# Third stage: the two rotary parts of the keys added by an accumulating transfer on GpSimd's queue

## The chip, the cores and the metric

The kernel runs on one core of one Trainium2 chip. The metric is the device time of one launch in microseconds (us).

## The reference

Three parts follow each other, on 64 sequences of 64 tokens of 128 numbers: a self-attention with 16 heads, a cross-attention on a context with a padding mask, and a stack of six layers (the third stage here). The change is in the stack's attention:

```python
def attn_layer(x, Wqkv, qs, ksc, Wo):
    q, k, v = jnp.split(x @ Wqkv, 3, -1)          # 16 heads of 64 each
    q = l2norm(q) * qs
    k = l2norm(k) * ksc
    q = q * cos * scale + rotate_half(q) * sin * scale
    k = k * cos * inv + rotate_half(k) * sin * inv
    out = local_attention(q, k, v)                # window of 32, softmax
    return out.transpose(0, 2, 1, 3).reshape(b, n, INNER) @ Wo
...
for i in range(DEPTH):                            # 6
    x = attn_layer(shift_tokens(x), ...) + x
    x = ffn_layer(shift_tokens(x), ...) + x
```

What matters is the sum in the line of `k`: one product with the cosines plus one with the sines. The kernel writes the two products into two buffers and adds them.

## The kernel before

The 4096 tokens lie in 32 tiles of 128 (two sequences each). The third stage works through 32 tiles times 6 layers, so 192 tile-steps; `turns` runs 192 + 7 turns, and in turn i every engine works at tiles i, i-1, ... down to i-7, each at another step of the chain. Each engine has its own `turn` function, which lists its steps in a fixed order; the engines meet by semaphores alone. Nothing is planned at run time, so an engine that waits at one step holds back all that stand behind it in its list.

The way of one tile's keys through the stage, with the lines of the kernel before:

- TensorE, `queries_keys` (L1044, matmuls at L1041): four 128x512 products, two of them keys, into PSUM.
- ScalarE, `squares` (L1248), then VectorE, `squares_summed` (L1361) and `seeded` (L1369 to L1373): the sums of squares by head and a first guess at the inverse roots.
- VectorE, `rotary` (L1346): the products with cosines and sines, from PSUM into `R[:, KEYS, 0, :]` and `R[:, KEYS, 1, :]`, each 128 x 1024 fp32. It counts `s.rotated`.
- GpSimd, `inverse_lengths` (L1494 to L1502): three Newton steps on 32 columns, each instruction waiting for the one ahead of it.
- GpSimd, `keys_added` (L1451): two additions of 128x512 that put the second part onto the first.
- GpSimd, in its next turn, `keys_scaled` (L1459): two multiplications of 128x512 by the inverse lengths, in place.
- TensorE, in its next turn, `keys_turned` (L1062, transposes at L1014), and ScalarE's `keys_out` (L1222); then the scores.

GpSimd's list of a turn is this, and its order is the order of its queue:

```python
keys_scaled(i - 1, k - 1, 0)
keys_scaled(i - 1, k - 1, 1)
scores_scaled(i - 2, k - 2, 0)
probs_scaled(i - 3, k - 3, 0)
scores_scaled(i - 2, k - 2, 1)
probs_scaled(i - 3, k - 3, 1)
inverse_deviation(i - 5, k - 5)
inverse_lengths(i, k)
keys_added(i, 0)
keys_added(i, 1)
```

`scores_scaled` (L1465) and `probs_scaled` (L1471) are multiplications of 128x512 for the softmax of older tiles: ScalarE's `exponents` (L1261) wait for the first, TensorE's `probs_turned` for the second. `inverse_deviation` (L1478 to L1483) makes the factors of the feed-forward's normalisation, for which ScalarE's `normalised` (L1271) waits; it needs VectorE's `statistics` (L1356). `R` has one buffer: VectorE's next key products wait until TensorE has turned the old ones (`s.k_turned`).

The transfers of the third stage are issued by SyncE: per tile-step six of 16 to 32 KB between SBUF buffers (`ystat`, `ys`), and once in each layer the weights of the next. GpSimd issues no transfer.

Of the kernel before, what the change touches and what calls it, by code (L numbers as in the profile page):

```python
# [24 lines left out]
ALU = mybir.AluOpType  # L25
# [26 lines left out]
def hold(eng, held):  # L52


    eng.sem_inc(held, 1)
# [818 lines left out]
QUERIES, KEYS = 0, 1  # L874
# [4 lines left out]
def turns(eng, turn, n):  # L879

    for i in range(n + LAST):
        turn(i, i % 4)


def inside(t, n):

    return not isinstance(t, int) or 0 <= t < n
# [12 lines left out]
def local(nc, sem, m):  # L900
# [10 lines left out]
    s = Names()  # L911
# [29 lines left out]
    with nc.Block() as block:  # L941
# [494 lines left out]
        @block.gpsimd  # L1436
        def _(pool):
            tt = nc.gpsimd.tensor_tensor

            def wide(small):  # L1440
                return small.unsqueeze(2).to_broadcast([128, 8, HD])

            def by_head(ap):
                return ap.rearrange("p (n k) -> p n k", k=HD)

            def keys_added(t, j):
                if inside(t, N):
                    if j == 0:
                        pool.wait_ge(s.rotated, 4 * t + 4)
                    at = slice(j * 512, (j + 1) * 512)  # L1450
                    tt(m.R[:, KEYS, 0, at], m.R[:, KEYS, 0, at], m.R[:, KEYS, 1, at], ALU.add).then_inc(s.k_added, 1)  # L1451

            def keys_scaled(t, k, j):
                if inside(t, N):
                    pool.wait_ge(s.k_added, 2 * t + j + 1)
                    if j == 0:
                        pool.wait_ge(s.lengths, 12 * t + 12)
                    part = by_head(m.R[:, KEYS, 0, j * 512:(j + 1) * 512])
                    tt(part, part, wide(m.rn[:, k % 4, 16 + 8 * j:24 + 8 * j]), ALU.mult).then_inc(s.k_scaled, 1)  # L1459

            def scores_scaled(t, k, a):
                if inside(t, N):
                    pool.wait_ge(s.less, 2 * t + a + 1)
                    part = by_head(m.P[:, k % 2, a * 512:(a + 1) * 512])
                    tt(part, part, wide(m.rn[:, k % 4, a:16:2]), ALU.mult).then_inc(s.scaled, 1)  # L1465

            def probs_scaled(t, k, a):
                if inside(t, N):
                    pool.wait_ge(s.inverse, 2 * t + a + 1)
                    part = by_head(m.P[:, k % 2, a * 512:(a + 1) * 512])  # L1470
                    tt(part, part, wide(m.inv_sum[:, k % 2, 8 * a:8 * a + 8]), ALU.mult).then_inc(s.normal, 1)  # L1471

            def inverse_deviation(t, k):
                if inside(t, N):
                    one = slice(k % 2, k % 2 + 1)
                    pool.wait_ge(s.var, t + 1)
                    hold(pool, held)
                    nc.gpsimd.tensor_scalar(m.vare[:, :], m.mv[:, k % 2, 1:2], EPS, None, ALU.add).then_inc(s.vare, 1)  # L1478
                    pool.wait_ge(s.vare, t + 1)
                    tt(m.rstd[:, one], m.vare[:, :], m.minus_half[:, :], ALU.pow).then_inc(s.pow, 1)  # L1480
                    pool.wait_ge(s.pow, t + 1)
                    hold(pool, held)
                    nc.gpsimd.tensor_scalar(m.nmr[:, one], m.mv[:, k % 2, 0:1], m.rstd[:, one], -1.0, ALU.mult, ALU.mult)\  # L1483
                        .then_inc(s.rstd, 1)

            def inverse_lengths(t, k):
                if inside(t, N):
                    pool.wait_ge(s.seed, 3 * t + 3)
                    y = m.seed[:, k % 2, :].bitcast(FP32)
                    for step in range(3):  # L1490
                        done = 12 * t + 4 * step
                        if step:
                            pool.wait_ge(s.lengths, done)
                        tt(m.rn_a[:, :], y, y, ALU.mult).then_inc(s.lengths, 1)  # L1494
                        pool.wait_ge(s.lengths, done + 1)
                        tt(m.rn_b[:, :], m.rn_a[:, :], m.ssm[:, k % 2, :], ALU.mult).then_inc(s.lengths, 1)
                        pool.wait_ge(s.lengths, done + 2)
                        hold(pool, held)
                        nc.gpsimd.tensor_scalar(m.rn_a[:, :], m.rn_b[:, :], -0.5, 1.5, ALU.mult, ALU.add)\
                            .then_inc(s.lengths, 1)  # L1500
                        pool.wait_ge(s.lengths, done + 3)
                        tt(m.rn[:, k % 4, :], y, m.rn_a[:, :], ALU.mult).then_inc(s.lengths, 1)  # L1502
                        y = m.rn[:, k % 4, :]

            def turn(i, k):
# [5 lines that stand above are left out]
                probs_scaled(i - 3, k - 3, 1)  # L1511
                inverse_deviation(i - 5, k - 5)
                inverse_lengths(i, k)
                keys_added(i, 0)
                keys_added(i, 1)

            turns(pool, turn, N)


# [48 lines left out]
```

## Time and profile before

| | |
|---|---|
| median of 2 runs | 3672.97 us (3669.88 to 3676.06) |
| the profiled execution | 3669.16 us |
| its span, first to last instruction | 3667.4 us |
| TensorE busy | 3570.1 us (97%) |
| VectorE, ScalarE, GpSimd busy | 2809.8, 2926.9, 2596.7 us |
| mean granted TensorE clock | 0.991 of 2.4 GHz |

The profiled execution's own time and its span differ by 1.8 us. Busy time doesn't say which engine sets the end: an engine at 97% may be held by another, and one at 71% may be the one that all wait for in some stretch. For that the waits, the chain that ended last and the order of one turn have to be read. In the rows, PE is TensorE, PEld its weight loads, DVE VectorE, ACT ScalarE, POOL GpSimd, SP SyncE and SPq SyncE's DMA queue.

### The profile page before, as it was taken

What the parts mean: (1) busy time and instruction counts of PE and PEld (TensorE: products, weight loads), DVE (VectorE), ACT (ScalarE), POOL (GpSimd) and SP (SyncE); (2) the same over time, 40 slices, a digit from 0 to 9 for tenths busy, and PEclk for the clock granted to TensorE, in tenths of its full rate; (3) what the DMA queues carried; (4) which work ended last, traced back from release to release, by engine and by line L of the source; (5) the groups of instructions that cost most, each with busy time, mean ns of one, the idle gap of its engine ahead of it and who ended that gap; (6) DMA issues with size and microseconds to landing.
All of it is one profiled execution on the core that took longest, in us unless ns stands there. A gap on an engine that the chain in (4) does not pass through costs nothing.

```text
span 3667.4 us, 125829 instructions
## 1 busy us (share of the span) xinstructions
PE 3570.1 (97%) x51141; PEld 2636.6 (72%) x51141; DVE 2809.8 (77%) x5297; ACT 2926.9 (80%) x5539; POOL 2596.7 (71%) x4812
## 2 busy tenths in 40 slices
PE   6989997999999999999999999999999999999997
PEld 5778874677777777777777777777777777777776
DVE  5834446788888888888888888888888888888884
ACT  5756664788888888888888888888888888888886
POOL 4622225778777787777877777777777777777773
PEclk9999999999999999999999999999999999999998
DMA  3000000000001000000000010000000000000000
GB/s 98 3 10 9 8 5 15 21 11 10 10 16 26 18 10 9 11 25 25 10 10 11 16 26 18 10 11 11 25 25 10 11 11 16 14 13 13 16 13 14
DMA packets 145114, 59.13 MB, mean 16 GB/s; under 512 B 117018, under 2 KB 139295, under 8 KB 144543
## 3 DMA queue, kind: packets, MB, share of 16 engines
q1 hardware_dynamic: 144542, 51.08, 5.6%
q8 instruction: 412, 6.75, 0.8%
q14 instruction: 160, 1.30, 0.1%
HBM read 23.95 MB, written 2.10 MB: 7 GB/s over the span
## 4 chain that ended last, share of the span: by engine, by line
PE 81%; DVE 1%; POOL 1%; ACT 0%; issue 0%; DMA 0%; SPq 0%; POOLq 0%; DVEq 0%
PE bank L1041 18%; PE bank L1014 11%; PE bank L1188 10%; PE bank L1093 10%; PE bank L1156 7%; PE bank L1172 6%; PE bank L1124 5%; PE bank L1109 5%; PE bank L1126 4%; PE bank L1032 3%; PE bank L1104 2%; DVE R L1346 0%; DVE ss L1361 0%; DMA ys<-Y 0%; POOL R L1459 0%
## 5 line engine op out<-in xcount | busy, mean ns | idle before, releaser
L1346 DVE TENSOR_TENSOR R<-bank,tables 128x1024 f32<-128x1024 f32 x768 | 903.6, 1218 | 218.6 <-ACT sq L1248 218.3
L1041 PE MATMUL bank<-WA,xcT 128*128 128x512 f32 x1536 | 693.9, 594 | 4.3 <-ACT xcT L1222 2.4
L1248 ACT ACTIVATE sq<-bank 128x512 f32<-128x512 f32 x768 | 459.3, 598 | 159.1 <-PE bank L1041 159.1
L1451 POOL TENSOR_TENSOR R<-R 128x512 f32<-128x512 f32 x384 | 481.6, 1277 | 0.0
L1041 PEld LDWEIGHTS bank<-WA,xcT 128*128 128x128 f32 x1536 | 277.2, 190 | 283.2 <-issue 279.5
L1361 DVE TENSOR_REDUCE ss<-sq 128x16 f32<-128x1024 f32 x384 | 459.8, 1198 | 0.2 <-issue 0.2
L1093 PE MATMUL bank<-WV,xcT 128*64 128x512 f32 x1536 | 414.2, 618 | 0.0
L1465 POOL TENSOR_TENSOR P<-P,rn 128x512 f32<-128x512 f32 x384 | 404.5, 1054 | 0.0
L1471 POOL TENSOR_TENSOR P<-P,inv_sum 128x512 f32<-128x512 f32 x384 | 404.0, 1052 | 0.7 <-DVE inv_sum L1401 0.7
L1188 PE MATMUL bank<-WO,OT 128*128 128x128 f32 x3072 | 397.1, 283 | 0.0
L1459 POOL TENSOR_TENSOR R<-R,rn 128x512 f32<-128x512 f32 x384 | 393.4, 1048 | 0.0
L1188 PEld LDWEIGHTS bank<-WO,OT 128*128 128x128 f32 x3072 | 360.6, 193 | 13.0
L1124 PE MATMUL bank<-ident,R 128*128 128x128 f32 x1536 | 356.5, 280 | 0.0
L1126 PE MATMUL bank<-ident,R 128*128 128x128 f32 x1536 | 345.8, 273 | 0.0
L1222 ACT ACTIVATE V<-bank 128x512 f32<-128x512 f32 x384 | 231.5, 603 | 81.8 <-PE bank L1093 81.8
L1156 PE MATMUL bank<-xnT,W 128*128 128x128 f32 (+1 forms) x2304 | 289.6, 276 | 1.7 <-DVE Y L1330 1.7
L1222 ACT ACTIVATE qT<-bank 128x512 f32<-128x512 f32 x384 | 229.9, 599 | 59.4 <-PE bank L1126 55.5
L1014 PEld LDWEIGHTS bank<-ident,P 128*128 128x128 f32 x1536 | 165.0, 142 | 154.3 <-issue 153.8
L1478 POOL TENSOR_SCALAR vare<-mv 128x1 f32<-128x1 f32 x192 | 42.7, 223 | 320.2 <-DVE mv L1356 320.1
L1156 PEld LDWEIGHTS bank<-xnT,W 128*128 128x128 f32 (+1 forms) x2304 | 266.3, 180 | 2.4 <-ACT xnT L1238 2.4
L1014 PEld LDWEIGHTS bank<-ident,R 128*128 128x128 f32 x1536 | 179.3, 141 | 103.2 <-issue 100.1
L1291 ACT ACT_TABLE_LOAD x192 | 246.3, 1283 | 3.5
(157 smaller groups left out, 7815.5 us busy)
## 6 DMA issues: line engine op xcount, KB each, us to landing
WA<-in_wqkv SPq DMA_DIRECT2D x24, 256.0 KB, 2.9
ystat<-Y SPq DMA_DIRECT2D x192, 32.0 KB
ystat<-Y SPq DMA_DIRECT2D x384, 15.8 KB
ys<-Y SPq DMA_DIRECT2D x192, 32.0 KB
ys<-Y SPq DMA_DIRECT2D x384, 15.8 KB
WV<-in_wqkv SPq DMA_DIRECT2D x6, 512.0 KB, 3.8
WO<-in_wo SPq DMA_DIRECT2D x6, 512.0 KB, 4.4
X<-in_x SPq DMA_DIRECT2D x4, 512.0 KB, 5.2
```

Source lines behind the costliest of these rows:

```text
L1014: return nc.tensor.transpose(dst, src, m.ident[:, :])
L1041: mm(b[QK_BANK[n, half]][:, :], m.xsT[:, k % 2, :], cols[:, half, :, :], start=True, stop=True)\
L1093: last = mm(V_BANK[bb][64 * e:64 * e + 64, :], m.xsT[:, k % 2, bb * 64:bb * 64 + 64], cols[:, e, :, :], start=True, stop=True)
L1124: mm(QT_BANK[j][:, col:col + 128], m.R[:, QUERIES, 0, at:at + 128], m.ident[:, :], is_transpose=True, start=True, stop=False)
L1126: last = mm(QT_BANK[j][:, col:col + 128], m.R[:, QUERIES, 1, at:at + 128], m.ident[:, :], is_transpose=True, start=False, stop=True)
L1156: last = mm(FF_BANK[c][0:rows, side * 128:(side + 1) * 128], m.W1[:, off + at:off + at + rows], m.xnT[:, k % 2, :], start=True, stop=True)
L1188: last = mm(OUT[:, 0:128], m.OT[:, k % 2, at:at + 128], flat(wo[:, :, c * 128:(c + 1) * 128]), start=(c == 0), stop=(c == PAIRS - 1))
L1222: return nc.scalar.activation(dst, src, ACT.Copy)
L1248: nc.scalar.activation(by_half[:, half, :, :], b[QK_BANK[n, half]][:, :].rearrange("p (h d) -> p h d", d=32), ACT.Square)\
L1346: tt(both, src.unsqueeze(1).to_broadcast([128, 2, 16, 32]), tab.unsqueeze(2).to_broadcast([128, 2, 16, 32]), ALU.mult).then_inc(s.rotated, 1)
L1361: nc.vector.tensor_reduce(m.ss[:, k % 2, 16 * n:16 * n + 16], m.sq[:, n, :].rearrange("p (h d) -> p h d", d=HD), AX.X, ALU.add)\
L1451: tt(m.R[:, KEYS, 0, at], m.R[:, KEYS, 0, at], m.R[:, KEYS, 1, at], ALU.add).then_inc(s.k_added, 1)
```

## The change

`keys_added` issues one transfer from SBUF to SBUF on GpSimd's queue, in which the second part is added onto the first, 128 x 1024 fp32 (512 KB), in place of the two additions. `keys_scaled`, at the head of GpSimd's next turn, waits once for the transfer's semaphore (16 counts for each transfer) in place of two waits for the additions' counts. The places of both steps in GpSimd's list stay.

```diff
-            def keys_added(t, j):
+            def keys_added(t):
+                if inside(t, N):
+                    pool.wait_ge(s.rotated, 4 * t + 4)
+                    pool.dma_start(m.R[:, KEYS, 0, :], m.R[:, KEYS, 1, :], accum_op=ALU.add).then_inc(s.k_added, 16)
+
+            def keys_scaled(t, k, j):
                 if inside(t, N):
                     if j == 0:
-                        pool.wait_ge(s.rotated, 4 * t + 4)
-                    at = slice(j * 512, (j + 1) * 512)
-                    tt(m.R[:, KEYS, 0, at], m.R[:, KEYS, 0, at], m.R[:, KEYS, 1, at], ALU.add).then_inc(s.k_added, 1)
-
-            def keys_scaled(t, k, j):
-                if inside(t, N):
-                    pool.wait_ge(s.k_added, 2 * t + j + 1)
-                    if j == 0:
+                        pool.wait_ge(s.k_added, 16 * t + 16)
                         pool.wait_ge(s.lengths, 12 * t + 12)
                     part = by_head(m.R[:, KEYS, 0, j * 512:(j + 1) * 512])
                     tt(part, part, wide(m.rn[:, k % 4, 16 + 8 * j:24 + 8 * j]), ALU.mult).then_inc(s.k_scaled, 1)
...
                 inverse_lengths(i, k)
-                keys_added(i, 0)
-                keys_added(i, 1)
+                keys_added(i)
```

## Rows read from the trace of the kernel before

**Rows 1.** The page's first part: busy time of each engine over the whole span.

```profile
PE 3570.1 (97%) x51141; PEld 2636.6 (72%) x51141; DVE 2809.8 (77%) x5297; ACT 2926.9 (80%) x5539; POOL 2596.7 (71%) x4812
```

**Rows 2.** Windows: stretch, length, each engine's busy time, PE clock, DMA share, GB/s.

```profile
0.00:157.00 157.00, 127.70 (x2675) 93.51 (x2676) 112.46 (x249) 100.77 (x241) 87.50 (x196) 1.00 0.20 58
157.00:325.00 168.00, 153.96 (x2783) 125.23 (x2783) 79.17 (x175) 100.00 (x204) 49.94 (x92) 0.96 0.03 9
...
700.00:1200.00 500.00, 500.00 (x6815) 364.73 (x6814) 407.44 (x759) 424.51 (x791) 395.08 (x729) 1.00 0.06 15
```

**Rows 3.** The waits between 700 and 3500 us: total us, times, longest us.

```profile
POOL vare L1478 <- DVE mv L1356: 271.6, 177, 1.9
...
ACT xn L1271 <- POOL nmr L1483: 102.2, 177, 0.9
...
POOL rn_a L1494 <- DVE seed L1373: 51.1, 174, 0.6
```

**Rows 4.** GpSimd's timeline, one turn: start us, us, engine, line, operation, count.

```profile
2002.28 2.04 POOL L1459 TENSOR_TENSOR R<-R,rn 128x512 f32<-128x512 f32 x2
2004.28 1.05 POOL L1465 TENSOR_TENSOR P<-P,rn 128x512 f32<-128x512 f32 x1
...
2006.29 1.05 POOL L1465 TENSOR_TENSOR P<-P,rn 128x512 f32<-128x512 f32 x1
2007.29 1.04 POOL L1471 TENSOR_TENSOR P<-P,inv_sum 128x512 f32<-128x512 f32 x1
2009.87 0.22 POOL L1478 TENSOR_SCALAR vare<-mv 128x1 f32<-128x1 f32 x1 [1.53 <-DVE mv L1356]
...
2010.95 0.27 POOL L1483 TENSOR_SCALAR nmr<-mv,rstd 128x1 f32<-128x1 f32 x1 [0.21 <-POOL rstd L1480]
2011.55 0.24 POOL L1494 TENSOR_TENSOR rn_a<-seed 128x32 f32<-128x32 f32 x1 [0.33 <-DVE seed L1373]
...
2015.42 0.25 POOL L1502 TENSOR_TENSOR rn<-rn,rn_a 128x32 f32<-128x32 f32 x1
2015.63 2.51 POOL L1451 TENSOR_TENSOR R<-R 128x512 f32<-128x512 f32 x2
2018.10 2.05 POOL L1459 TENSOR_TENSOR R<-R,rn 128x512 f32<-128x512 f32 x2
```

**Rows 5.** All instructions of L1451: min/median/max ns, first and last start.

```profile
L1451 POOL TENSOR_TENSOR R<-R x384: 1262/1278/1291, 591.7 to 3598.4; 128x512 f32<-128x512 f32 x192
```

**Rows 6.** DMA issues of the page: count, KB each, median us from issue to landing.

```profile
WA<-in_wqkv SPq DMA_DIRECT2D x24, 256.0 KB, 2.9
...
WV<-in_wqkv SPq DMA_DIRECT2D x6, 512.0 KB, 3.8
WO<-in_wo SPq DMA_DIRECT2D x6, 512.0 KB, 4.4
```

**Rows 7.** DMA issues, whole list: smaller transfers, and a store of 256 KB.

```profile
ctx_sb<-in_ctx_in SPq DMA_DIRECT2D x32, 64.0 KB, 1.8
out<-X SPq DMA_DIRECT2D x8, 256.0 KB, 2.4
```

**Rows 8.** SyncE's issue instruction of the 512 KB transfer: min/median/max ns.

```profile
L267 SPq DMA_DIRECT2D WV<-in_wqkv x6: 378/379/432, 29.5 to 3089.1; - x6
```

**Rows 9.** TensorE's timeline of the same turn.

```profile
2007.41 1.04 PE L1014 MATMUL bank<-ident,R 128*128 128x128 f32 x8
2008.37 1.08 PE L1093 MATMUL bank<-WV,xcT 128*64 128x512 f32 x4
...
2013.56 1.09 PE L1014 MATMUL bank<-ident,P 128*128 128x128 f32 x8
```

**Rows 10.** ScalarE's timeline of the same turn.

```profile
2009.06 1.16 ACT L1261 ACTIVATE P<-P 128x512 f32<-128x512 f32 x2
...
2011.25 0.49 ACT L1271 ACTIVATE xn<-ys,nmr,rstd 128x128 f32<-128x128 f32 x1 [0.55 <-POOL nmr L1483]
```

**Rows 11.** VectorE's timeline of the same turn: the seeds and the key products.

```profile
2011.29 0.18 DVE L1373 TENSOR_SCALAR seed<-bits 128x32 int32<-128x32 int32 x1
2011.38 2.35 DVE L1346 TENSOR_TENSOR R<-bank,tables 128x1024 f32<-128x1024 f32 x2
```

## The prediction

> **What bounds the kernel now.** I read the busy times first. TensorE is at 97%, GpSimd at 71% [rows 1]. By stretches, the third stage stands out: between 700 and 1200 us TensorE is busy 500.00 of 500 us at the full granted clock, GpSimd 395 us [rows 2], and the four stretches of 500 us behind it read the same. So in the steady part TensorE sets the pace and no other engine ever stops it. The waits agree: in the list of the third stage no large wait of TensorE on another engine stands; what stands there are waits of the others [rows 3]. GpSimd itself waits for VectorE, 271.6 us in 177 turns for the variance and 51.1 us for the seeds: it has spare time, 1.5 + 0.3 us in a turn. A step that is taken off GpSimd therefore gains nothing by being gone. The whole question is whether what replaces it fits into GpSimd's turn.
>
> **How long a turn is.** The additions of the first tile start at 591.7 us and the second addition of the last at 3598.4 us [rows 5]. Taking off the one addition between (1.28), 191 turns take 3005.4 us, 15.74 us each.
>
> **What GpSimd's turn holds.** From the timeline of one turn [rows 4]: key scaling, score scaling and probability scaling run without a gap from 2002.28 to 2008.33 (6.05 us). A wait of 1.53 us follows. The deviation takes from 2009.87 to 2011.22 (1.35 us); a wait of 0.33 us; the inverse lengths from 2011.55 to 2015.67 (4.12 us, most of it latencies of a dependent chain, which don't shrink). Without waits and without the additions: 6.05 + 1.35 + 4.12 = 11.52 us. The additions hold 2.47 us more (2015.63 to 2018.10).
>
> **What the change does to it.** It removes those 2.47 us. It adds a transfer of 512 KB, issued where the additions stood, and a wait for its landing at the head of the next turn. The point to see: that wait is the very next entry of GpSimd's list. Nothing stands between issue and wait, so the transfer overlaps no GpSimd work at all; its whole time D from issue to landing takes the place of the 2.47 us. Behind the wait are queued both key scalings, both score scalings, both probability scalings, the deviation, the next inverse lengths, and the next transfer. TensorE waits for the keys and the probabilities, ScalarE for the scores and the deviation. GpSimd's turn can't be shorter than 11.52 + D, and the stage takes the longer of that and TensorE's 15.74 us. GpSimd becomes the bound from **D = 4.2 us** on; each us above costs about 191 us in all.
>
> Below that point nothing else would show, for the stretch that GpSimd may slip is large: the first keys are scaled by about 2003.3, TensorE turns them at 2007.41 [rows 4, 9]; the second score scaling ends at 2007.34 and ScalarE comes to its second exponent at about 2009.6 [rows 4, 10]; the probabilities are done by 2008.33 and turned from 2013.56 [rows 4, 9]. The one near consumer is ScalarE's normalisation, which already waits 0.55 us for GpSimd [rows 10]; but the deviation starts on VectorE's word, not on GpSimd's, until the slip has eaten the 1.53 us. The key products are ready before the issue: VectorE starts them at 2011.38 and ends near 2013.7, GpSimd comes at 2015.63 [rows 4, 11].
>
> **How long is D?** The trace of before has no transfer on GpSimd's queue and none that accumulates, so D is bounded by the nearest rows. A plain load of the same bytes on SyncE's queue lands 3.8 us after its issue; 256 KB take 2.9 us, and 512 KB in small pieces 4.4 us [rows 6]. 64 KB take 1.8 us [rows 7].
> - An addition has to read its destination as well as its source, so 1 MB is read for 512 KB written. The second read is priced by the slope between 256 and 512 KB, 0.9 us for 256 KB: +1.8 us. Ends: 0 (both reads side by side) and +4.4 (a whole second pass at the dearer row).
> - Both ends of the transfer lie in SBUF. The only row that hints at this is the store of 256 KB, 2.4 against the load's 2.9 us [rows 6, 7]: -0.5. Ends: -0.6 and 0.
> - The queue is GpSimd's, whose own cores must prepare the rows that SyncE issues in 0.38 us [rows 8]. Ends: 0, and 1.3 us, GpSimd's dearest instruction here [rows 5]. I take 0.9, nearer to the dear end, since a list for 128 partitions is wanted.
>
> Sum: 3.8 + 1.8 - 0.5 + 0.9 = **6.0 us**; by the low ends 3.2, by the high ones 9.5.
>
> The Trainium skill, "DMA: Bandwidth & Descriptors", section on the anatomy of one DMA on the gpsimd path, gives about 2.0 us fixed plus bytes over 436 GB/s: 3.2 us for 512 KB once, and if the second read counts in full 4.4 us (my estimate). By 3.2 the change would do nothing, by 4.4 it would cost about 35 us. The Trainium skill, "Collectives: The Full Stack", section on the bandwidth ceiling, says that an adding transfer runs at half the rate of a copy because of the second read; that speaks against the change and for counting twice, and no row here shows it. That the plain load here takes 3.8 and not 3.2 us is why I trust the rows.
>
> **Sum.** A turn of 11.52 + 6.0 = 17.52 us against 15.74: +1.78 us, times 191 = +340 us. On the profiled execution's own 3669.16 that makes 4009; its time stands 3.8 us below the median, so against the median about **4013 us**, 9.3% slower. At 17.5 us the other chains fit: from the first scaled half of the keys, TensorE needs 15.8 us to come back to the same step, about 1 us more since the second half comes later, and some 0.7 us since ScalarE's late normalisation delays the copies of the queries: about 17.5, so it arrives at about the time when the keys do. The granted clock costs nothing: with TensorE busy 81% of the first stretch it was 1.00, at 92% in the second 0.96 [rows 2], and TensorE is then not the bound.
>
> **The rivals.** Within 2%, which is about what a measurement of this kernel can tell from no change, lies 73 us, or 0.38 us a turn.
> - *The transfer fits* (not slower). D stays under 4.2 us because the destination is read beside the source and the fixed part between SBUF buffers is small: 1.8 us for 64 KB plus the store's slope (0.6 us for 192 KB) over 448 KB gives 3.2 us [rows 7]. Then GpSimd's waits for VectorE shrink and TensorE goes on at 100%: 3673 us. To 4.6 us it remains within 2%: up to 3746. For it: that slope. Against: it lies under the load row of equal size, and allows nothing for the addition or for GpSimd's own part. The formula of the Trainium skill's "DMA: Bandwidth & Descriptors" quoted above is the same claim, and gives the same 3.2.
> - *The addition is a bottleneck in the transfer* (far slower). If the adding itself halves the rate twice over, or the pass is repeated, D is 4.4 + 4.4 = 8.8 us, or more with GpSimd's part: a turn of 20.3, +4.6 us, 4550 us. For it: no row shows an addition in a transfer. Against: each of the sixteen engines has only 32 KB of it.
> - *Faster.* Less GpSimd traffic to SBUF could shorten VectorE's or TensorE's instructions. TensorE's steady part has no gap to close, so this is under 1 in 50.
> - *The change doesn't do what it says*: if the wait let GpSimd pass early, time would be as in the first rival; the count of 16 by transfer speaks against it.
>
> **How the numbers follow.** Main case, D from 4.6 to 8 us (3746 to 4395): 0.72. Transfer fits or nearly: 0.15. Bottleneck beyond 8 us: 0.11. Faster: 0.02. So slower by over 2%: 0.83, within: 0.15, faster: 0.02. The range holds 8 in 10: from 3670 (the case without change is near and cheap to include) to 4370, D = 7.85 us.
>
> **What would show it.** Right: GpSimd's largest wait is the one of key scaling (L1459's successor) for the transfer, about 6 us less the issue in each of 192 turns; its waits for the variance and the seeds are gone; TensorE waits for scaled keys at the transposes, its busy share falls to about 89% (3570 of 4009); two key scalings in successive turns start 17.5 us apart. Wrong: that distance is 15.7 and GpSimd's waits for VectorE remain in part; or the distance isn't 11.52 + D with the D that the trace shows, which would mean that another chain binds. The term most likely mis-sized is D, and in it the second read and GpSimd's own preparation.

## The result, and the profile after

The changed kernel takes 3858.94 us (median of 2 runs) against 3672.97 us: ratio 1.0508, 95% interval 1.0491 to 1.0525, so 5.1% slower. In the experiments below a ratio compares with executions of the kernel before from the same session (medians 3670.28 to 3671.64 us). One execution, of the dead transfer with one SBUF input, ran at a granted clock of 0.683 (4921.61 us) and is left out of its ratio. The profiled execution took 3858.59 us, with a span of 3856.8 us, 189.4 us more than before.

The page of the changed kernel, its busy times, the chain that ended last (shares of the span by engine), and the new transfer (192 issues, KB each, median us from issue to landing); the last line has all its landings:

```profile
PE 3639.3 (94%) x51141; PEld 2635.9 (68%) x51141; DVE 2940.2 (76%) x5297; ACT 2877.7 (75%) x5539; POOL 2295.5 (60%) x4620
...
POOL 47%; DMA 25%; issue 10%; PE 1%; POOLq 0%; DVE 0%; ACT 0%; SPq 0%; DVEq 0%
...
R<-R POOLq DMA_DIRECT2D x192, 512.0 KB, 4.9
...
DMA to landing us min/median/max: 4.5/4.9/7.9
```

Against [rows 1], GpSimd is *less* busy (60% where it was 71%), and yet the chain that ended last now runs through GpSimd and through the transfer `R<-R`; TensorE has 1% of it. The engine that sets the pace here spends much of its time waiting, and its busy share doesn't tell. The windows show that TensorE has gaps now (500.00 of 500 us before, [rows 2]) at the same full clock:

```profile
700.00:1200.00 500.00, 481.19 (x6462) 342.45 (x6461) 408.01 (x716) 392.36 (x746) 324.17 (x650) 1.00 0.23 45
```

The waits of the changed kernel between 700 and 3600 us (total us, times, longest us):

```profile
POOL R L1457 <- DMA R<-R: 727.3, 173, 7.0
...
ACT xn L1271 <- POOL nmr L1481: 236.9, 173, 1.7
...
ACT P L1261 <- POOL P L1463: 166.3, 172, 1.2
...
PE bank L1014 <- ACT qT L1222: 85.3, 171, 1.0
PEld bank L1014 <- POOL R L1457: 78.6, 149, 2.9
...
PE bank L1014 <- POOL R L1457: 20.5, 55, 2.1
```

GpSimd's waits for VectorE, the first and third of [rows 3], are no longer listed; one wait for the transfer has taken their place, 4.2 us in each turn. ScalarE and TensorE wait for GpSimd. One turn on GpSimd:

```profile
2010.45 0.95 POOL L1449 DMA_DIRECT2D R<-R  x1
2015.87 2.04 POOL L1457 TENSOR_TENSOR R<-R,rn 128x512 f32<-128x512 f32 x2 [4.47 <-DMA R<-R]
2017.87 1.04 POOL L1463 TENSOR_TENSOR P<-P,rn 128x512 f32<-128x512 f32 x1
...
2027.42 0.95 POOL L1449 DMA_DIRECT2D R<-R  x1
2032.31 2.04 POOL L1457 TENSOR_TENSOR R<-R,rn 128x512 f32<-128x512 f32 x2 [3.93 <-DMA R<-R]
```

Between issue and key scaling GpSimd does nothing. The additions took 2.47 us of its turn [rows 4]; issue and wait together take 4.9 to 5.4 us in these two turns, 5.16 us in the mean of the 147 turns that begin between 720 and 3180 us. All else in GpSimd's turn, from the start of the key scaling to the next issue, takes 11.55 us here (2015.87 to 2027.42) and 11.60 us in the mean of the same turns.

The length of a turn can be read from any instruction that occurs once in it. The first instruction of the deviation, between 720 and 3180 us, before and after (count, min/median/max ns, first and last start):

```profile
L1478 POOL TENSOR_SCALAR vare<-mv x155: 222/223/223, 728.8 to 3164.4; 128x1 f32<-128x1 f32 x155
```

```profile
L1476 POOL TENSOR_SCALAR vare<-mv x147: 230/258/263, 730.0 to 3176.8; 128x1 f32<-128x1 f32 x147
```

Before, (3164.4 - 728.8) / 154 = 15.82 us; after, (3176.8 - 730.0) / 146 = 16.76 us. That is 11.60 + 5.16, as it must be by the way in which the turn was divided; what the division shows is that GpSimd's own part has stayed at the 11.52 us of the forecast but for 0.08, so no other wait of weight has entered its turn. The whole loss: the first such instruction comes 12.8 us later (662.9 for 650.1; 1 to 2 of them stand already in the second stage, the others fall into the turns that fill this one), the last 188.8 us later (3840.7 for 3651.9), so 176 us fall on 191 turns, 0.92 each.

### The profile page after: what moved, and what is told of

Its sections match the earlier page's. It is cut to its first block, busy times and chain, and to the rows that moved or that the text cites. A ratio compares the mean times of both kernels' runs of the same rounds, so it can differ in the third digit from the quotient of the medians.

```text
span 3856.8 us, 125637 instructions
## 1 busy us (share of the span) xinstructions
PE 3639.3 (94%) x51141; PEld 2635.9 (68%) x51141; DVE 2940.2 (76%) x5297; ACT 2877.7 (75%) x5539; POOL 2295.5 (60%) x4620
## 4 chain that ended last, share of the span: by engine, by line
POOL 47%; DMA 25%; issue 10%; PE 1%; POOLq 0%; DVE 0%; ACT 0%; SPq 0%; DVEq 0%
DMA R<-R 25%; POOL R L1457 10%; POOL P L1469 9%; POOL P L1463 8%; POOL rn_b L1494 4%; POOL rn L1500 4%; POOL rn_a L1492 3%; POOL rn_a L1497 3%; POOL rstd L1478 3%; POOL vare L1476 1%; POOL nmr L1481 1%; POOLq L55 0%; PE bank L1188 0%; DMA ys<-Y 0%; PE bank L1041 0%
## 5 line engine op out<-in xcount | busy, mean ns | idle before, releaser
L1261 ACT ACTIVATE P<-P 128x512 f32<-128x512 f32 x384 | 242.8, 633 | 183.0 <-POOL P L1463 183.0
L1124 PE MATMUL bank<-ident,R 128*128 128x128 f32 x1536 | 356.4, 279 | 0.0
L1126 PE MATMUL bank<-ident,R 128*128 128x128 f32 x1536 | 345.8, 273 | 0.0
L1014 PE MATMUL bank<-ident,P 128*128 128x128 f32 x1536 | 246.2, 284 | 92.1 <-ACT qT L1222 92.1
L1271 ACT ACTIVATE xn<-ys,nmr,rstd 128x128 f32<-128x128 f32 x192 | 94.7, 493 | 276.7 <-POOL nmr L1481 276.7
L1014 PE MATMUL bank<-ident,R 128*128 128x128 f32 x1536 | 219.7, 278 | 33.0 <-POOL R L1457 31.4
L1382 DVE TENSOR_REDUCE mx<-bank 128x8 f32<-128x512 f32 x384 | 245.5, 681 | 6.1 <-PE bank L1109 6.1
## 6 DMA issues: line engine op xcount, KB each, us to landing
ystat<-Y SPq DMA_DIRECT2D x384, 15.8 KB
ys<-Y SPq DMA_DIRECT2D x384, 15.8 KB
```

Of the source, the lines that this page charges most:

```text
L1014: return nc.tensor.transpose(dst, src, m.ident[:, :])
L1124: mm(QT_BANK[j][:, col:col + 128], m.R[:, QUERIES, 0, at:at + 128], m.ident[:, :], is_transpose=True, start=True, stop=False)
```

## The experiments

Theory A is the forecast's: a turn is the longer of TensorE's 15.8 us and GpSimd's 11.6 us plus whatever of the transfer lies bare between issue and use. Rival B: the transfer's traffic, or its issue, slows the other engines, and the wait only shows it. Theory C came up on the way.

**The addition left out of the transfer** (the keys are the second part alone).

```diff
-pool.dma_start(m.R[:, KEYS, 0, :], m.R[:, KEYS, 1, :], accum_op=ALU.add).then_inc(s.k_added, 16)
+pool.dma_start(m.R[:, KEYS, 0, :], m.R[:, KEYS, 1, :]).then_inc(s.k_added, 16)
```

> Changed kernel with the accumulation left out of the transfer (the keys are then the second part alone), all else the same. It prices the second read within the transfer's 5.1 us from issue to the next key scaling. Theory A (the turn of GpSimd is 11.55 us plus the exposed time of the transfer, or TensorE's 15.74 if that is longer): a turn of 11.55 plus whatever the copy takes; if the second read costs 0.9 us or more, the copy takes at most 4.2 us and the time is 3673 to 3690 us; if the addition is free, nothing changes and the time is 3859. Theory B (the traffic of the transfer slows other engines, the wait is not what costs): about 3859, or some 60 us below for a third less traffic, with the wait still there.

3706.08 us, one run; turn 15.97 us. Issue and landings (instruction: min/median/max ns; the second line in us):

```profile
L1449 POOL DMA_DIRECT2D R<-R x192: 604/642/762, 594.4 to 3629.7; - x192
...
DMA to landing us min/median/max: 2.9/4.1/6.1
```

From issue to use the copy takes 4.18 us in the mean (120 turns), 0.98 less than with the addition. That is the price of the addition, and 0.3 us of it lies in the issue itself (0.64 for 0.95). Theory A's sum of means, 11.6 + 4.18 = 15.8, says no loss, and its expectation was at most 3690, so it missed by 16 us. The spread can account for that: a landing of 6 us delays the turn, one of 3 us gives nothing back while TensorE sets the pace. In 97 of the 192 turns issue to use took more than 4.22 us; these excesses add up to 66 us, and some 34 were lost. That the spread is the whole cause isn't shown.

**Half the bytes** (the second halves of the keys are not added).

```diff
-pool.dma_start(m.R[:, KEYS, 0, :], m.R[:, KEYS, 1, :], accum_op=ALU.add).then_inc(s.k_added, 16)
+pool.dma_start(m.R[:, KEYS, 0, 0:512], m.R[:, KEYS, 1, 0:512], accum_op=ALU.add).then_inc(s.k_added, 16)
```

> Changed kernel with an accumulating transfer of the first 512 columns only, 256 KB (the second halves are not added). It splits the transfer's time into a fixed part and a part by bytes. Theory A: with 5.1 us for 512 KB and 0.9 us for each 256 KB read twice, so 1.8 us less, 3.3 us from issue to use; the turn is TensorE's 15.74 us, the time 3673 us, and a wait of 0.5 to 2.5 us is left. Theory B: half the traffic, half the loss: about 3765 us.

3689.01 us, one run; turn 15.87 us. Neither theory's number is met exactly, A's (3673) by 0.4%, B's (3765) by 2%. The waits between 700 and 3500 us, and the landings:

```profile
POOL R L1457 <- DMA R<-R: 557.5, 177, 6.1
```

```profile
DMA to landing us min/median/max: 3.3/4.0/6.9
```

The wait is 557.5 / 177 = 3.15 us; with the issue of 0.95, 4.10 us for 256 KB (3.3 were expected) against 5.16 for 512 KB. So 256 KB more, source and destination read, cost 1.06 us; if the first 256 KB cost as much, 3.0 us are fixed (an estimate from these two sizes). A mean of 4.10 is just under the 4.2 us from which GpSimd sets the pace.

**A dead transfer beside the additions.** The kernel before, plus the same accumulating transfer between two spare buffers.

```diff
+def dead_transfer(t):
+    if inside(t, N):
+        at_least(pool, s.dead, 16 * t)
+        pool.dma_start(m.dead[:, 0, :], m.dead[:, 1, :], accum_op=ALU.add).then_inc(s.dead, 16)
...
 keys_added(i, 1)
+dead_transfer(i)
```

> Kernel before, its two additions kept, plus the same accumulating transfer of 512 KB in each tile-step between two spare buffers that nobody reads; nothing but the next such transfer waits for it. Theory A: GpSimd's turn is 11.52 + 2.47 + 0.95 for the issue = 14.94 us, under 15.74; time 3673 us, within 0.3%. Theory B (traffic or issue slow the others): up to 3859 us, visibly above 3690.

3767.61 us, ratio 1.0257 (1.0240 to 1.0274). That speaks against A as it stood. The same counting of turns, by stretch, shows where the time went:

```profile
L1486 POOL TENSOR_SCALAR vare<-mv x156: 230/232/233, 721.3 to 3173.0; 128x1 f32<-128x1 f32 x156
...
L1486 POOL TENSOR_SCALAR vare<-mv x16: 230/232/233, 3262.8 to 3554.1; 128x1 f32<-128x1 f32 x16
```

In the first five layers a turn takes (3173.0 - 721.3) / 155 = 15.82 us, as before, with all the traffic: there rival B is out. In the last layer it takes 19.42 us, 3.6 us more. Only the last layer has VectorE's addition of the finished tile to X (L1334 before, L1337 here). That instruction in this kernel, and in the kernel before:

```profile
L1337 DVE TENSOR_TENSOR X<-X,Y x32: 291/4130/5305, 3215.0 to 3764.6; 128x128 f32<-128x128 f32 x32
```

```profile
L1334 DVE TENSOR_TENSOR X<-X,Y x32: 291/952/1058, 3206.5 to 3664.4; 128x128 f32<-128x128 f32 x32
```

Beside it GpSimd runs its four scalings; the timeline of this kernel in the last layer:

```profile
3506.69 1.32 POOL L1473 TENSOR_TENSOR P<-P,rn 128x512 f32<-128x512 f32 x1
...
3507.08 4.07 DVE L1337 TENSOR_TENSOR X<-X,Y 128x128 f32<-128x128 f32 x1
...
3507.69 1.31 POOL L1479 TENSOR_TENSOR P<-P,inv_sum 128x512 f32<-128x512 f32 x1
...
3508.69 1.31 POOL L1473 TENSOR_TENSOR P<-P,rn 128x512 f32<-128x512 f32 x1
...
3509.70 1.30 POOL L1479 TENSOR_TENSOR P<-P,inv_sum 128x512 f32<-128x512 f32 x1
```

VectorE's 0.29 us of work (the shortest of the 32) starts at 3507.08 and ends at 3511.15, just behind the last of GpSimd's scalings (3511.00). So it goes in 26 of the 32 additions: each is drawn out to 2.8 us or more, and ends 0.16 us behind the last scaling and 1.2 to 2.7 us after the transfer has landed, so it isn't the transfer that holds it. 26 turns of 3.6 us more make up the loss of 96 us. Each of GpSimd's scalings starts 1.00 us after the one ahead but lasts 1.30: they overlap. In the kernel before they last 1.04 to 1.05 us at the same spacing [rows 4], and by its 0.95 us VectorE gets in after one of them. Theory C: GpSimd shut VectorE's instruction with two inputs in SBUF out until its whole row of instructions was through.

**The dead transfer, with one SBUF input** (in the last layer the feed-forward result alone is added to X, straight from PSUM and ahead of the addition to Y; the rest of Y is left out of the output, and VectorE's wait between the two additions goes too).

```diff
-tt(y, y, FF_OUT[:, 0:128], ALU.add).then_inc(s.y, 1)
 if layer(t) == DEPTH - 1:
-    dve.wait_ge(s.y, t + 1)
-    tt(x, x, y, ALU.add).then_inc(s.final, 1)
+    tt(x, x, FF_OUT[:, 0:128], ALU.add).then_inc(s.final, 1)
+tt(y, y, FF_OUT[:, 0:128], ALU.add).then_inc(s.y, 1)
```

> The kernel before with the dead transfer, but in the last layer VectorE adds the feed-forward result to X straight from PSUM (one input in SBUF, one in PSUM) ahead of the addition to Y, where it added X and Y, both in SBUF. The rest of Y is left out of the output by it. The dead transfer cost 96 us, all of it in the last layer, where that addition took 4.1 us in place of 0.95. Theory C (GpSimd's instructions, which follow one another without a gap behind the issue, shut VectorE's instruction with two SBUF inputs out, and the traffic itself costs nothing): the 96 us are gone, 3665 to 3685 us. Theory B (traffic, in some other way that only the last layer feels): still about 3768 us.

3674.68 us, ratio 1.0012 (1.0002 to 1.0021); the addition to X, same kernel otherwise:

```profile
L1335 DVE TENSOR_TENSOR X<-X,bank x32: 286/287/289, 3210.2 to 3667.4; 128x128 f32<-128x128 f32 x32
```

The 96 us are gone, but for some 0.1%, with the scalings still overlapping (1.30 us). Theory C holds, and with it the traffic and the issue of 192 transfers are shown to cost next to nothing by themselves: what costs is who waits. The Trainium skill, "SBUF — State Buffer", section "Who interferes with whom", has the rule that an instruction of VectorE with two SBUF inputs contends with GpSimd's reads, and the later one is held until the first is through. These rows agree for single instructions (0.95 for 0.29 us before); that a whole row of GpSimd's instructions counts as one when they overlap (4.13 us) goes beyond it.

**The key scalings moved behind the four other scalings**, so that work lies between issue and wait.

```diff
-keys_scaled(i - 1, k - 1, 0)
-keys_scaled(i - 1, k - 1, 1)
 scores_scaled(i - 2, k - 2, 0)
 probs_scaled(i - 3, k - 3, 0)
 scores_scaled(i - 2, k - 2, 1)
 probs_scaled(i - 3, k - 3, 1)
+keys_scaled(i - 1, k - 1, 0)
+keys_scaled(i - 1, k - 1, 1)
```

> Changed kernel with the two key scalings moved behind the four scalings of scores and probabilities in GpSimd's turn, so that 4.1 us of work stand between the issue and the wait. Theory A: of the 5.1 us only 0.95 for the issue and 0 to 0.3 us of wait remain exposed; GpSimd's turn is 12.5 to 12.8 us, TensorE sets the pace again, time 3670 to 3690 us (ratio 1.00). The keys then come at about the time when TensorE wants them, so up to 0.3 us a turn (60 us) may remain. Theory B: unchanged, about 3859 us.

3711.81 us, ratio 1.0109 (1.0094 to 1.0124): 147 of the 186 us come back, a little less than expected (3690 at most). The turn is 15.92 us in the first layers and (3552.0 - 3276.3) / 17 = 16.22 us in the last. The waits that are left between 700 and 3500 us:

```profile
POOL R L1457 <- DMA R<-R: 87.6, 101, 2.3
PEld bank L1014 <- POOL R L1457: 47.4, 132, 1.5
```

The longer landings still come too late, and TensorE now wants the keys at once. In the last layer theory C shows again: the four scalings now follow the issue without a wait and overlap, the first two lasting 1.35 and 1.16 us in one turn, and VectorE's addition to X takes up to 2.79 us.

```profile
L1476 POOL TENSOR_SCALAR vare<-mv x18: 230/231/233, 3276.3 to 3552.0; 128x1 f32<-128x1 f32 x18
...
L1334 DVE TENSOR_TENSOR X<-X,Y x32: 291/624/2786, 3238.1 to 3707.3; 128x128 f32<-128x128 f32 x32
```

**The issue moved ahead of the third Newton step.**

```diff
 for step in range(3):
+    if step == 2:
+        keys_added(t)
...
 inverse_lengths(i, k)
-keys_added(i)
```

> Changed kernel with the wait for the products and the issue moved ahead of the third Newton step of the inverse lengths, so that 1.4 us of GpSimd's work lie between issue and wait. Theory A: of some 5.1 us from issue to use, 3.7 stay exposed; GpSimd's turn is 11.6 + 3.7 = 15.3 us, just under TensorE's 15.8; time 3675 to 3710 us, the upper end since the transfer's time varies from turn to turn. Theory B (traffic): about 3859 us.

3679.15 us, ratio 1.0021 (1.0012 to 1.0031); turn 15.83 us. The transfer itself is as slow as before (5.13 us from issue to use, 121 turns), and GpSimd still waits for it in every turn between 700 and 3500 us, 2.8 us each:

```profile
POOL R L1457 <- DMA R<-R: 502.4, 177, 4.7
```

But 1.4 us of cover alone bring nearly the whole loss back, since GpSimd's turn falls to 11.6 + 5.13 - 1.4 = 15.3 us.

**Both moves.**

> Both moves together: issue ahead of the third Newton step, key scalings behind the four other scalings, so 5.5 us of GpSimd's work between issue and wait. Theory A: the transfer is covered whole, only its issue of 0.95 us is paid; GpSimd's turn is 12.5 us, TensorE's 15.8 sets the pace, time 3670 to 3685 us: as before, not faster, since TensorE has no gap to give. Theory B: about 3859 us. If VectorE's last-layer addition is shut out as with the dead transfer, up to 3770 us.

3678.44 us, ratio 1.0022 (1.0012 to 1.0032); turn (3177.0 - 725.3) / 155 = 15.82 us in the first layers, and the same in the last. GpSimd waits for the transfer once, 0.5 us, in the 177 turns between 700 and 3500 us:

```profile
L1476 POOL TENSOR_SCALAR vare<-mv x156: 230/232/233, 725.3 to 3177.0; 128x1 f32<-128x1 f32 x156
...
POOL R L1457 <- DMA R<-R: 0.5, 1, 0.5
```

In the steady part the hidden transfer costs nothing, and no gain stands behind it. Of the 13.7 us by which the span of this profiled execution is longer than that of the kernel before, 12.4 stand already at the stage's first deviation, half of them before the first transfer.

**Four additions and no transfer.**

```diff
+def keys_again(t, j):
+    if inside(t, N):
+        at = slice(j * 512, (j + 1) * 512)
+        tt(m.dead[:, j, :], m.R[:, KEYS, 1, at], m.R[:, KEYS, 1, at], ALU.add)
...
 keys_added(i, 1)
+keys_again(i, 0)
+keys_again(i, 1)
```

> Kernel before with two more additions of 128x512 on GpSimd behind the two of the keys (their result goes to a spare buffer), no transfer at all. Theory A: GpSimd's turn is 11.6 + 4.95 = 16.55 us with no transfer in it, so about 0.75 us a turn above TensorE's 15.8: 3673 + 143 = 3815 us, and more, to 3910, if the last layer's addition on VectorE is shut out. Theory B (the loss comes from the transfer's traffic): about 3673 us.

3729.36 us, one run: less than A's number, far above B's. GpSimd's timeline gives the reason:

```profile
2002.77 2.50 POOL L1452 TENSOR_TENSOR R<-R 128x512 f32<-128x512 f32 x2
2005.23 2.04 POOL L1457 TENSOR_TENSOR dead<-R 128x512 f32<-128x512 f32 x2
2007.23 2.05 POOL L1465 TENSOR_TENSOR R<-R,rn 128x512 f32<-128x512 f32 x2
```

The extra pair, which reads one buffer twice, takes 2.00 us and not 2.47. With that, 11.60 + 2.46 + 2.00 = 16.06 us; the turn measured 16.03. The expectation had priced the extra pair at 2.47 us. So a longer GpSimd turn slows the kernel with no transfer in it. VectorE's addition to X took 0.76 us (median) there, though GpSimd works without a gap: its instructions don't overlap.

**The copy on SyncE's queue** (the sum left out), issued on the products' count.

```diff
+sp.wait_ge(s.rotated, 4 * t + 4)
+sp.dma_start(m.R[:, KEYS, 0, :], m.R[:, KEYS, 1, :]).then_inc(s.k_added, 16)
```

> A plain copy of the second part onto the first (the sum is left out), 512 KB, issued by SyncE as soon as the products are there, with nothing in its place on GpSimd. It prices GpSimd's queue: the same copy took 4.1 us from its issue there. By the terms of the forecast the copy takes 3.3 us here. It starts 1.9 us earlier than GpSimd would issue it, so theory A expects it hidden: 3665 to 3690 us. Theory B (traffic): 3706 us, as the copy on GpSimd's queue.

3675.34 us, one run; turn 15.82 us. From SyncE's issue to GpSimd's use 3.33 us in the mean (121 turns). GpSimd waits for the landing in every turn, 242.8 us in 177 turns between 700 and 3500 us, so the use follows the landing, and the turn stays TensorE's all the same. Thus GpSimd's queue costs 4.18 - 3.33 = 0.85 us more for the same copy.

**Half by the transfer, half by GpSimd**, the added half scaled first.

```diff
+pool.dma_start(m.R[:, KEYS, 0, 512:1024], m.R[:, KEYS, 1, 512:1024], accum_op=ALU.add).then_inc(s.k_added, 16)
+tt(m.R[:, KEYS, 0, 0:512], m.R[:, KEYS, 0, 0:512], m.R[:, KEYS, 1, 0:512], ALU.add).then_inc(s.k_half, 1)
```

> Changed kernel with half of the columns (256 KB) in the accumulating transfer and the other half added by GpSimd behind the issue and scaled first, so that 2.3 us of GpSimd's work lie behind the issue. Theory A: 4.0 us from issue to landing less 0.95 + 2.3 leaves 0.75 us of wait; GpSimd's turn is 11.6 + 0.95 + 1.25 + 0.75 = 14.5 us, under 15.8: 3670 to 3690 us. Theory B (traffic): 3689 us, as the half transfer alone.

3674.64 us, ratio 1.0010 (1.0000 to 1.0019); turn 15.82 us. As expected of A. No version tried beats the kernel before.

## Why the prediction was right, and by how much it was off

**The mechanism was the one named.** The transfer's time replaces the additions in a turn of GpSimd that has nothing to put between issue and wait; beyond some 4.2 us GpSimd takes the pace from TensorE. GpSimd's own part of the turn stayed at 11.60 us (11.52 forecast), so no other chain binds. Work put in between brings the time back, traffic alone costs nothing in the first five layers, and a longer GpSimd turn without a transfer costs what it should.

**The size was off.** +340 us were forecast and +186 came. GpSimd's own part was right (11.52 forecast, 11.60 measured), and so was the threshold: TensorE's turn is 15.82 us in the steady part where the forecast had 15.74, which leaves 4.2 us either way. The mis-sized term is D, 6.0 us against 5.16. Its parts, by the runs: the plain copy between SBUF buffers on SyncE's queue, 3.8 - 0.5 = 3.3 forecast, 3.33 measured; GpSimd's own queue, +0.9 forecast, +0.85 measured; the second read with the addition, **+1.8 forecast, +0.98 measured**, 0.3 of it in the issue. That the first two terms came out so close is in part luck: the -0.5 was taken from a store, whose row is no transfer between SBUF buffers, and the 0.9 was chosen between 0 and 1.3 us. The third step is the one that failed: the slope of a load from HBM (0.9 us for 256 KB, [rows 6]) was laid on a second read between SBUF buffers, doubled for 512 KB. The half transfer shows that 256 KB more cost 1.06 us with both reads together. Since a turn is lost only above 4.2 us, an error of 0.84 us in D (14%) made one of nearly half in the loss. The range, 3670 to 4370 us, would have held almost any time from no change upward; what the forecast can claim is the mechanism.

The fixed time plus bytes of the Trainium skill's "DMA: Bandwidth & Descriptors", section "Anatomy of one DMA — SWDGE (gpsimd) path", quoted in the forecast, gives 3.2 us for one pass, and is told there of GpSimd's path. Here SyncE's copy (3.33) comes near it and GpSimd's plain copy (4.18) doesn't; with the addition the forecast's estimate of 4.4 stands against 5.16. The half rate of an adding transfer, which the forecast also quotes, is told there of rings between cores; the runs here can neither confirm nor refute it, since the plain copy was timed at one size only, and so its time by bytes isn't known.

**The rivals.** The fitting transfer fell with D at 5.16; the bottleneck in the adding was not there (0.98 us). Nothing became faster. GpSimd did wait for the landing (727.3 us in 173 turns), so the change did what it says.

**The signs.** Right: the wait at the key scaling, the vanished waits for VectorE, ScalarE's late normalisation (236.9 us of wait for 102.2), and TensorE's wait for the queries' copies (0.5 us a turn, 85.3 / 171, for 0.7 forecast). That TensorE's wait comes from the late normalisation alone isn't shown, since ScalarE also waits for the score scalings (166.3 us). TensorE's share fell to 94%, not 89%, by the same error in D.

**What stays open.** Single transfers take from 4.5 to 7.9 us to land, 5.06 in the mean of 192. The four that are issued together with the weights of a next layer take 6.2 to 7.9 us; seven others above 6 us have no such neighbour, and what makes them long wasn't found. The plain copy and the half transfer lose 0.5 to 1% though their means would fit; that the spread is why is argued, not shown.

## What to carry to other kernels

A transfer that stands in for an engine's work relieves it only if other work of that engine lies between issue and wait: count what is queued between the two, and if it is nothing, the whole way from issue to landing (5.2 us for 512 KB here) goes into the engine's turn. Look for the engine that waits, not for the one that is busy; here GpSimd's busy share fell from 71% to 60% as it took over the pace. Where a loss begins at a threshold, the uncertainty of the difference is what counts, and a price between SBUF buffers is better not taken from a row of HBM where it can be measured.

## What the runs showed of the hardware that wasn't expected

- GpSimd's instructions of 128x512 that follow a transfer's issue without a wait between last 1.30 us at a spacing of 1.00 and overlap; then a VectorE addition with two SBUF inputs waits for the whole row (4.13 us, median) where it waits for one otherwise (0.95). The overlap stands in every run in which such instructions follow an issue without a wait (the dead transfer; the moved key scalings; half and half, whose additions last 1.57 us for 1.27) and in no other, the gapless four additions included (1.05). What in the issue causes it is not shown.
- VectorE's small instructions ahead of the seeds are held by GpSimd too. In the changed kernel 159 of the 192 take over 0.3 us, and each of these ends 0.04 us behind one of GpSimd's scalings of 128x512; in the kernel before two do. Their group (count, busy us, mean ns, idle before), after and before:

```profile
L1369 DVE TENSOR_SCALAR ssm<-ss 128x32 f32<-128x32 f32 x192 | 121.5, 633 | 6.7
```

```profile
L1369 DVE TENSOR_SCALAR ssm<-ss 128x32 f32<-128x32 f32 x192 | 35.3, 184 | 6.6
```

  VectorE has 0% of the chain that ended last, so they cost nothing here.
- The issue of an accumulating transfer of 512 KB occupies GpSimd 0.95 us, that of 256 KB as long, that of a plain copy 0.64 us.
